# Scale additions moved to ACT and DVE, a new order of the stream, x tiles ahead of w1, ten weight groups by way of a DRAM copy

## What is computed

```
x = x + layernorm(running_mean(layernorm(x)))          # running mean over the tokens
y = layernorm(x)
h      = gelu([y, mean(slots)] @ w1 + b1)              # 4096 x 512
logits = (h @ w2 + b2) / (|tau| + 0.1)                 # 64 slots
alpha  = softmax of the 8 largest logits, 0 elsewhere  # 4096 x 64
si     = (alpha.T @ y) / sum(alpha)                    # 64 x 1024
S_new  = GRU(si, slots; Wih, Whh)
S_new -> q, k, v, 64 x 64 attention, residual, layernorm, @ wvp, @ wo
x = x + layernorm(alpha @ that)
```

## Time and profile before

| | |
|---|---|
| median of 3 runs | 337.25 us (336.62 to 337.45) |
| profiled execution | 337.41 us; span of its slowest core (core 3) 335.9 us, 1.5 us lie around it |
| spans of the 8 cores | 321.7 to 335.9 us |
| busy, core 3 | PE 213.9, DVE 194.2, POOL 178.6, ACT 161.5 us |
| DMA, core 3 | 62.27 MB; the software (casting) queue takes 43.1% of the engines' span for 22.22 MB, the hardware queue 35.4% for 39.13 MB |
| HBM | read 67.35 MB, written 22.02 MB |

### The profile page before, as it was taken

The page is one execution under the profiler, slowest core; times in us unless marked ns, Lnnn a source line. Parts: engine busy times, 40 slices in busy tenths (PEclk is TensorE's granted clock), DMA queues, the critical chain, the costliest instruction groups (busy, mean ns, idle before and its releaser), DMA issues.

```text
span 335.9 us, 5678 instructions; the slowest of 8 cores (321.7 to 335.9 us)
## 1 busy us (share of the span) xinstructions
PE 213.9 (64%) x1726; PEld 125.2 (37%) x1726; DVE 194.2 (58%) x347; ACT 161.5 (48%) x268; POOL 178.6 (53%) x310
## 2 busy tenths in 40 slices
PE   0044066977698897979877888574225486588830
PEld 0011034645376673756755677531121132011100
DVE  0451568468998688686865665332310501899980
ACT  0044042456478584793865964413001012999940
POOL 8275187477588888798888873010000000555640
PEclk9999567899999999999999999958555557555555
DMA  6899999999996399979088007299999500599997
GB/s 163 185 166 203 240 274 230 258 220 236 250 242 181 110 191 171 112 106 178 18 101 152 4 0 127 39 208 194 212 214 274 152 0 0 224 346 349 353 415 315
DMA packets 24239, 62.27 MB, mean 185 GB/s; under 512 B 1894, under 2 KB 2406, under 8 KB 24210
## 3 DMA queue, kind: packets, MB, share of 16 engines
q0 software_dynamic: 11376, 22.22, 43.1%
q1 hardware_dynamic: 12032, 39.13, 35.4%
q10 hardware_dynamic: 802, 0.57, 0.7%
HBM read 67.35 MB, written 22.02 MB: 266 GB/s over the span
## 4 chain that ended last, share of the span: by engine, by line
DVE 25%; PE 25%; DMA 19%; POOL 11%; issue 11%; ACT 5%; DVEq 0%; POOLq 0%; ACTq 0%; SPq 0%
DVE sb_x L842 11%; DMA x1b<-wbf 9%; PE R L363 7%; DMA w1a_s<-w1a 6%; DMA sb_x<-x 4%; PE R L656 3%; DVE sb_x L328 3%; PE R L347 3%; POOL x3b_s L340 3%; PE R L807 2%; PE R L304 2%; DVE xT L355 2%; PE R L309 2%; PE R L467 2%; POOL x1b L295 2%
## 5 line engine op out<-in xcount | busy, mean ns | idle before, releaser
L363 PE MATMUL R<-xT,w1a_s 128*128 128x256 bf16 x512 | 67.0, 279 | 5.0 <-ACT gh L475 2.5
L363 PEld LDWEIGHTS R<-xT,w1a_s 128*128 128x128 bf16 x512 | 50.0, 100 | 15.8 <-issue 7.2
L328 DVE SCALAR_TENSOR_TENSOR sb_x<-R,sqs,sb_x 128x1024 f32<-128x1024 f32 x32 | 40.7, 1280 | 25.1 <-POOL sqs L325 25.0
L332 ACT ACTIVATE junk<-sb_x,nm 128x1024 bf16<-128x1024 f32 x32 | 36.7, 1148 | 36.0 <-DVE sb_x L328 34.4
L340 POOL TENSOR_SCALAR x3b_s<-sb_x,nm,vr 128x1024 bf16<-128x1024 f32 x32 | 38.6, 1207 | 9.1 <-POOL vr L339 2.7
L318 ACT ACTIVATE junk<-R 128x1024 bf16<-128x1024 f32 x32 | 32.7, 1023 | 18.3 <-PE R L314 17.5
L842 DVE SCALAR_TENSOR_TENSOR sb_x<-R,sqs,sb_x 128x1024 f32<-128x1024 f32 x32 | 38.8, 1284 | 3.5 <-POOL sqs L840 3.5
L295 POOL TENSOR_SCALAR x1b<-sb_x,nm,r 128x1024 bf16<-128x1024 f32 x32 | 38.6, 1208 | 1.9 <-POOL r L289 1.0
L826 PE MATMUL R<-svd,aT 64*128 64x512 bf16 x64 | 30.1, 608 | 11.0 <-DVE sb_x L842 8.4
L834 ACT ACTIVATE x1b<-R 128x1024 bf16<-128x1024 f32 x32 | 32.7, 1023 | 5.4 <-PE R L826 2.4
L304 PE MATMUL R<-x1b,cmat 128*128 128x512 bf16 x60 | 18.7, 394 | 20.7 <-DVE sb_x L328 19.0
(11 more groups left out here) (153 smaller groups left out, 329.6 us busy)
## 6 DMA issues: line engine op xcount, KB each, us to landing
sb_x<-x SPq DMA_DIRECT2D x16, 1024.0 KB, 22.3
out<-sb_x SPq DMA_DIRECT2D x32, 512.0 KB, 8.9
wbf<-wmid POOLq DMA_DIRECT2D x5, 1024.0 KB, 17.2
sb_x<-whh POOLq DMA_DIRECT2D x4, 1024.0 KB, 60.7
wsl<-wmid POOLq DMA_DIRECT2D x4, 1024.0 KB, 14.5
msl<-wmid POOLq DMA_DIRECT2D x3, 1024.0 KB, 15.6
msl<-wbf SPq DMA_DIRECT2D x3, 1024.0 KB, 29.5
wsl<-whh POOLq DMA_DIRECT2D x2, 1024.0 KB, 94.1
```

The source lines that it names most:

```text
L328: kx2[j] = DV.put(lambda v: v.scalar_tensor_tensor(xs(j), RR[j % 2][:], s2[:, j:j + 1], xs(j), op0=OP.mult, op1=OP.add), ks2[j], kx1[j])
L332: kv[j] = AC.put(lambda a: a.activation(junk[:], xs(j), AF.Square, bias=nm[:, j:j + 1], accum_out=vr[:, j:j + 1]), kx2[j], tt.get("junk"))
L363: PE.quiet(lambda e, jc=jc, dc=dc, ob=ob, q=q: e.matmul(ob, w1a[:, dc * H + jc * P:dc * H + (jc + 1) * P], xT[:, dc * 2 * P:(dc + 1) * 2 * ...
```

## The change

ORDER is replaced by another list of 31 steps with other offsets (`slot_in` now at -10 and -9, `logits` at -3, one `trans` at -3, `cumsum` at 1 and 2). Three kinds of small POOL instruction go: the addition for r becomes a DVE instruction, the addition after `sq_c` and the scaling and addition after `sq_x` become ACT instructions (Identity with a bias operand) right behind the Square. x tiles 0 to 7 are queued on SP without a wait, tiles 0 and 1 as loads of their own; w1a, and with it every later instruction of POOL, waits for tile 1; tiles 8 and up wait for w1a. CAST_AT now lists all groups 3 to 12, in turns 7 to 14. (last_h also takes the later half of the hidden layer.)

```
 ORDER = [
+    ("make_x2", -1), ("trans", -3), ("logits", -3), ("sq_c", 0), ("slot_in", -10), ("slot_in", -9),
+    ("make_x3", -2), ("evac_t", -3), ("top", -3), ("stats", 6), ("cumsum", 1), ("sq_x", -1),
+    ("scale2", 0), ("hidden_a", -2), ("shift", -3), ("exps", -3), ("sq_c", 1), ("hidden_b", -2),
+    ("make_x3", -1), ("stats", 7), ("gelu_a", -2), ("scale2", 1), ("trans", -2), ("make_x1", 3),
+    ("gelu_b", -2), ("make_x1", 4), ("make_x2", 0), ("cumsum", 2), ("weigh", -3), ("sq_x", 0),
+    ("evac_t", -2),
 ]
...
-        load_x(0, 2)
+        load_x(0, 1)
+        load_x(1, 1)
         load_x(2, 2)
+        load_x(4, 2)
+        load_x(6, 2)
...
+        keps = PO.put(lambda g: g.memset(eps[:], EPS))
...
-        kw1a = group("w1a", w1a[:], w1a_d)
+        kw1a = group("w1a", w1a[:], w1a_d, xin[1])
...
-        load_x(4, 2, kw1a)
-        for a in range(6, 24, 2):
+        load_x(8, 2, kw1a)
+        for a in range(10, 24, 2):
...
-            t = PO.put(lambda g: g.tensor_scalar(r1[:, a:j + 1], mvp[:, :, 1], EPS, 1.0,
-                                                 op0=OP.add, op1=OP.mult), kag[j])
+            t = DV.put(lambda v: v.tensor_scalar(r1[:, a:j + 1], mvp[:, :, 1], EPS, None, op0=OP.add), kag[j])
...
+            kq[j] = AC.put(lambda a: a.activation(s2[:, j:j + 1], sq[:, j:j + 1], AF.Identity, bias=c_e2[:, j:j + 1]),
+                           kq[j], ke2)
...
-            t = PO.put(lambda g: g.tensor_tensor(s2[:, j:j + 1], sq[:, j:j + 1], c_e2[:, j:j + 1], op=OP.add),
-                       kq[j], ke2)
+            t = kq[j]
...
+            kv[j] = AC.put(lambda a: a.activation(r3[:, j:j + 1], vr[:, j:j + 1], AF.Identity, scale=1.0 / D,
+                                                  bias=eps[:]), kv[j], keps)
...
-            t = PO.put(lambda g: g.tensor_scalar(r3[:, j:j + 1], vr[:, j:j + 1], 1.0 / D, EPS,
-                                                 op0=OP.mult, op1=OP.add), kv[j])
...
-        CAST_AT = {7: (4, 6), 9: (8,), 12: (10, 11)}
+        CAST_AT = {7: (3,), 8: (4,), 9: (5,), 11: (6, 7), 12: (8,), 13: (9, 10), 14: (11, 12)}
...
-        last_h = khA[NP - 1]
+        last_h = khB[NP - 1]
```

More of the change, by code:

```diff
@@ L165, in _build @@
         half = sbt("half", [P, 4])
+        eps = sbt("eps", [P, 1])
         tmp = sbt("tmp", [P, 8])
@@ L334, in sq_x @@
             tt["junk"] = kv[j]
+            kv[j] = AC.put(lambda a: a.activation(r3[:, j:j + 1], vr[:, j:j + 1], AF.Identity, scale=1.0 / D,
+                                                  bias=eps[:]), kv[j], keps)
         def make_x3(j):
-            t = PO.put(lambda g: g.tensor_scalar(r3[:, j:j + 1], vr[:, j:j + 1], 1.0 / D, EPS,
-                                                 op0=OP.mult, op1=OP.add), kv[j])
-            t = PO.put(lambda g: g.tensor_tensor(r3[:, j:j + 1], r3[:, j:j + 1], half[:, 0:1], op=OP.pow), t)
+            t = PO.put(lambda g: g.tensor_tensor(r3[:, j:j + 1], r3[:, j:j + 1], half[:, 0:1], op=OP.pow), kv[j])
             kx3[j] = PO.put(lambda g: g.tensor_scalar(x3s(j), xs(j), nm[:, j:j + 1], r3[:, j:j + 1],
@@ L568, in _build @@
                     off -= 2
-                if (name, off) == ORDER[-1]:
+                if (name, off) == ("make_x1", 4):
                     for j in ((2 * i + 4, 2 * i + 5) if 2 * i + 4 < NPAIRED else
```

## The result

| | before | changed |
|---|---|---|
| median of 4 runs each, taken side by side | 336.94 us (336.62 to 337.45) | 354.13 us (353.31 to 359.12) |
| ratio | | 1.050 (95%: 1.047 to 1.054) |
| profiled execution, slowest core | 335.9 us, core 3 | 352.0 us, core 5 |
| spans of the 8 cores | 321.7 to 335.9 us | 344.0 to 352.0 us |

The forecast was 305.5 us. The changed kernel is 17.2 us slower than the one before. The ratios leave out executions in which the cores of one die ran longer at a lower granted clock, such as the one of 359.12 us here and one of 328.32 us further down. These are rows of the page of the changed kernel: groups by line, then DMA issues, then queues.

A forecast was written before the change was run, and what follows sets the result against it. POOL was taken to bound the stream. Head 12.7, lighter POOL 1, turns 4 to 14 7.8, tail 0 and middle 10.2 sum to 31.7; 337.4 less that is 305.7, and 0.2 less for the median 305.5 us; range 297 to 321.

The forecast's parts named there:

- the price of a cast: POOL's DMA queue: 5.9 us a member, so ten casts and two straight groups from 111 take 71 us, to 182.
- DMA becomes the wait: Whh late for its gates, or the cast queue late for group 2: 315.5 us, at most 322; chance 0.15.
- the slack of 6 us: End of the cast queue: the last two casts land by 190, group 2 behind them is needed at about 196.
- 12 us a group: Pace of Whh's groups beside x loads, used for w1a's landing and as an argument for DMA becoming the wait.
- Head: Start of the kernel: DVE's 9.8 us hole goes, bias row starts near 39.5 instead of 52.24; gain 12.7, bounds 10 and 16.
- Additions and order: Lighter POOL gains 1 us before turn 4; shorter double turns gain 7.8 in turns 4 to 14, bounds 0 and 14.
- Identity on ACT: Stream: eight one-column activations per double turn at 0.35 us each, 2.8 us together; 0.3 to 0.7 each thought possible.
- rival 3: Stream: each Identity needs a table load of 1.28 us, making the kernel slower at 362 us; chance 0.03.
- Gates: Stream: Whh's last half lands at 111, its product comes at 115; hidden by 4 us, beyond that one for one.
- Tail: End of the stream, from 189.07 to 220.85: gain 0, bounds 3 us either way.
- Middle: After the stream: nothing waits for weights, a middle of 52 us; gain 10.2, bounds 7 and 18.
- Output: Output part at the end of the kernel: not touched, time as before.

The follow-up runs named there:

- one of 328.32 us further down: An execution of the changed kernel with only groups 3 to 9 cast and the third Whh product in turn 10 instead of 9; median 323.61 us, ratio 0.955.
- the cut-down kernel: The kernel cut to DMA batches, x loaded and stored unchanged, nothing computed; six casts with rows of 4 KB took 58.6 us, 9.8 each.

## Why the prediction was wrong

**The step that failed** is the price of a cast, "land at 179.0 and 184.7, the second 5.7 us behind", and from it "12 x 5.9 = 71 us, to 182". The row is right, and so is the subtraction, but the two casts were issued within 0.8 us and ran side by side. The gap between two such landings is what the second still lacked when the first was in, not what a cast costs. The batch costs 17.2 + 0.8 = 18.0 us for two, 9.0 each, and that stood in the same rows. The longer batch of the cut-down kernel gives 9.8. By the prediction's own steps with 9.8 for a cast and 7.5 for a straight group: 111 + 98 + 15 + 7.5 = 231.5 for group 2, needed at 196: 35 us of wait, and 305.5 + 35 = 340.5, slower than before. Of the 13.6 us from there to 354.1 the queue has 13.3, as it ended at 244.8: 8.7 because Whh landed at 119.7 and not at 111, 4.6 over the prices above. The misses of the terms below, earlier in the kernel, went into the wait.

**The rival was there, at the wrong price.** "DMA becomes the wait: [...] the cast queue late for group 2" is what happened, at that place, with a chance of 0.15 and "Ten us late is 315.5, at most 322". The cap took the slack of 6 us, which rests on the failed price. A bound of a queue's price from both sides would have put 12 us a group (which the prediction quoted) on all thirteen members: 111 + 156 = 267.

**It was also counted as free.** The prediction gave a cast one issue on POOL and one fetch on SP. The write of the copy and its later read come on top of the straight read, which the megabytes of the queues don't show, and the line on HBM does.

Term by term:
- *Head*, 12.7 forecast. The bias row starts at 42.1, not 39.5: 10.2. POOL's wait for tile 1 let w1a out at 10.05, not 7.5, and w1b landed at 39.9. Turn 4 is 9.2 earlier, and the head alone brought 9.5. Right mechanism, 2.5 to 3 too large. Of the hole of 9.8 us on DVE 2.5 are left: the first instruction for tile 4 waits until 22.7, where the prediction had 21.
- *Additions and order*, 1 + 7.8. In the changed kernel 3.5 between turns 4 and 14. Without a gate the double turns are 19.0 and 19.4 (forecast 19.0), so the busy queues were sized right. With a gate the first took 20.5 for 20.0, with PE busy throughout at a mean granted clock of 0.88; in the kernel with the old head and casts the same double turn took 18.9 at 1.00 (core 1) and 20.5 at 0.92 to 0.94. The additions' share was misjudged: POOL as "the bound" would have to give a gain by itself, and what it gave, 0.7, can't be told from none. With the new order POOL waits less for what has moved.
- *Identity on ACT*, 0.35 each with its wait. The changed kernel has 0.294 us for each of the 64 and 3.0 us of idle time ahead of each 32, 0.39 together. The number of table loads stays at that of before, so rival 3 is out. The Trainium skill (ScalarE: Activation LUTs, "What ACT_TABLE_LOAD costs") gives about 280 ns for such an activation; the trace, at 294, agrees within 5%.
- *Gates*: the last half of Whh landed at 119.7, not 111, and PE waited 3.0 us for it in turn 9, which makes the double turn of 23.7. "Hidden by 4 us" was wrong by 7. Of the 8.7 us POOL's late w1a accounts for 2.5; the rest was not separated.
- *Tail*, 0 with 3 either way: +2.7.
- *Middle*, 52 without waits: 84.4 - 30.3 = 54.1, and 51.3 where seven casts were made. The 10.2 us could be had in the slowest core, by fewer casts.
- *Output*, as before: +4.2 between the two slowest cores, but 0.8 by the medians of the eight (54.8 and 55.6), so most of it is which core is the slowest. Core 3 before did its last stores at 420 GB/s, core 5 now at 351 to 356. The eight cores of the changed kernel end closer together (spans within 8 us, 14 before), which would load the memory more at once; that was not tested, and it stays open.

## What to carry to other kernels

Take the price of a DMA from a batch, its first issue to its last landing divided by its members, not from the gap between the landings of two that were issued together; and check it against the bytes that DRAM reads and writes for it, both legs of a copy. A queue in order is costed to its last member, with the time at which the one behind it is needed: one urgent transfer behind ten early ones inherits all of their time. When such a queue sets the end, gains elsewhere turn into waiting, so the first look at a change that adds transfers is the slack at the end of their queue. And a stretch is compared over all cores: 4.2 us in the output part of two slowest cores were 0.8 in the medians.

## What was not expected of the hardware

With all eight cores at work, transfers inside DRAM with rows of 4 KB ran at 307 to 322 GB/s of bytes read plus written per core, whatever was cast and whoever issued them: 9.8 to 10.2 us for a cast group, 6.6 for a bf16 copy, 13.5 for an f32 copy. Rows of 16 KB gave 337 GB/s, 9.3 us for 9.8, and POOL's issue took 0.50 us for 0.73. A fetch of 1 MB on SP's queue landed after 6.2 to 10.7 us in a batch of three with nothing beside it, and after 25.9 among two straight groups and other fetches. Double turns of the stream in which the mean granted clock was 0.92 to 0.94 instead of 1.00 took 1.1 to 1.7 us longer in most places; in the fourth double turn of the kernel before, where POOL was busy 18.1 of 20.95 us, they took no longer.
